# Three new homes for the moving operands of a float32r kernel: 96, 48 and 64 bytes behind a multiple of 128

## The chip, the cores and the metric

The kernel runs on one core of one Trainium2 chip. The metric is the device time of one execution in microseconds, the median of several runs. TensorE's granted clock is read from the profile; its two levels are 1.2 and 2.4 GHz.

## The reference

A stack of four layers over `x` of shape (2, 1024, 256), 2048 tokens of 256 features, with a context of 64 tokens per batch. Each layer is a gated cross attention and a gated feed-forward, both after a layer norm:

```
for layer in 0..3:
    x = x + g_xattn[layer] * cross_attention[layer](layernorm(x), ctx)
    x = x + g_ffn[layer]   * feed_forward[layer](layernorm(x))
```

The feed-forward of layers 0, 2 and 3 is a mixture of 8 experts with 256 -> 1024 -> 256 features (top 1 in layers 0 and 2, top 2 in layer 3), and routes tokens. That of layer 1 runs all 8 experts, each with a gate, an up and a down matrix, over all 2048 tokens. Inputs and outputs are float32.

## The kernel before

All weights of the feed-forwards are split into a high and a low half of type float32r, and so are the tokens and the activations. A float32 product is made of three matmuls in a row: high weights by high tokens, high weights by low tokens, low weights by high tokens. 7200 such matmuls are issued; the weights (128x128) are the stationary operand, and the tokens or activations are the moving operand.

- Layer 1 (`ffn1`): 32 units (8 experts by four quarters of the hidden features), each for two pairs of token blocks, so 64 groups. A group has 14 `product` calls of three matmuls (lines 950 to 952) and four calls of `down` for six matmuls (through the helper `mm`, line 689), 66 matmuls of 512 columns. `product` combines sums of blocks of the tokens with sums of blocks of the weights, seven products in place of eight. The sums of token blocks T2, T3 and T4 stand in `pair_x_rest`; T1 and the plain blocks stand in `xTh` and `xTl` (`x_operand`). `down` reads `h_hi` and `h_lo`.
- Layers 0, 2, 3 (`moe`): 15, 8 and 8 items, each with 8 chunks of the hidden features. A chunk has six matmuls up, which read `xTh`/`xTl`, and six down, which read `h_hi`/`h_lo`, with 256, 384 and 320 columns.

The order on TensorE within a group is written out by hand in `group`: products, `down`, products, `down`, products. PE waits there on semaphores of VectorE (`p_lo`, `p_sum`, `p_y`), ScalarE (`p_act`, `p_copy`) and GpSimd (`p_wup`, `p_wdown`). ScalarE writes `h_hi` (L1491) and VectorE writes `h_lo` (L1939 in layer 1, L2162 in the expert layers). VectorE adds L1926, L1935 (gate and up) and L1948 (the output sum).

All tiles are allocated in one order in each partition of the on-chip memory, each at the next multiple of 32 bytes. Their byte addresses modulo 128, here called homes, follow from that order: `wsplit` (the split weights) starts at 97312, home 32; `moving_home`, a tile of 32 bytes that nothing reads or writes, starts at 172800 (home 0) and pushes `xTh` to 172832; `xTl` follows at 189216, `h_act` at 205600, `h_hi` at 211744, `h_lo` at 219936, all home 32. `pair_x_rest` lies in `wsplit` behind the four blocks of weights, home 32 as well. `xT` stands at home 0 and `sc` at home 0.

Of the kernel before, what the change touches and what calls it, by code (L numbers as in the profile page):

```python
# [11 lines left out]
F32R = mybir.dt.float32r  # L12
# [5 lines left out]
P = 128  # L18
# [7 lines left out]
GT = GROUP * P  # L26
# [15 lines left out]
FH = 4  # L42
QUARTER = F // 4
UNITS = 4 * E
PAIRED = 2 * GT
# [7 lines left out]
UP_COLS, W_COLS = 7 * 2 * P, 7 * 2 * P + 2 * D  # L53
# [17 lines left out]
def build(nc, a, out, subs):  # L71
    with ExitStack() as ctx:
        def sb(name, shape, dt=F32, stack=ctx):
            return stack.enter_context(nc.sbuf_tensor(name, shape, dt))
# [28 lines left out]
        wsplit = sb("wsplit", [P, 16 * PIECE], F32R)  # L103
# [88 lines left out]
            q_inv = asb("q_inv", [P, 2, KD, GT])  # L192
            q_o = asb("q_o", [P, KD, GT])

        sb("moving_home", [P, 8])
        xTh = sb("xTh", [P, KD, T], F32R)
        xTl = sb("xTl", [P, KD, T], F32R)
        h_act = sb("h_act", [P, 2, GT])
        logit_rows = sb("logit_rows", [P, NG, P])
        h_hi = sb("h_hi", [P, FH, GT], F32R)  # L200
        h_lo = sb("h_lo", [P, FH, GT], F32R)

        pair_w = wsplit[:, 0:4 * W_COLS].rearrange("p (s h w) -> p s h w", s=2, h=2)
        pair_up = [[pair_w[:, z, h, 0:UP_COLS].rearrange("p (o m w) -> p o m w", o=7, m=2) for h in range(2)] for z in range(2)]
        pair_down = [[pair_w[:, z, h, UP_COLS:W_COLS].rearrange("p (i d) -> p i d", i=2) for h in range(2)] for z in range(2)]
        pair_x_rest = wsplit[:, 4 * W_COLS:4 * W_COLS + 6 * PAIRED].rearrange("p (h o t) -> p h o t", h=2, o=3)
        lnx_flat = lnx[:, :, :].rearrange("p t d -> p (t d)")
        kept23 = lnx_flat[:, 0:PAIRED].rearrange("p (m t) -> p m t", m=2)
        x_sums = lnx_flat[:, PAIRED:3 * PAIRED].rearrange("p (o t) -> p o t", o=4)
# [2116 lines left out]
```

## Time and profile before

| | |
|---|---|
| median of 3 runs | 1953.7 us (1948.84 to 1954.12) |
| the profiled execution | 1959.86 us |
| its span, first to last instruction | 1958.1 us |
| mean granted TensorE clock | 0.972 |
| TensorE busy | 1828.0 us |
| VectorE, ScalarE, GpSimd busy | 1401.2, 1093.2, 731.4 us |

The span is what the profile's times are counted in. Busy time is the union of an engine's instructions; a matmul's duration reaches from its start to its modelled end and is longer than the distance to the next matmul's start, since they are pipelined. The distance between starts is what a stream of matmuls costs.

### The profile page before, as it was taken

The numbers are of one execution on the slowest core, as the hardware profiler recorded it, in microseconds if no ns is written. First come the engines' busy times: TensorE is split into PE (matmuls) and PEld (weight loads), VectorE is DVE, ScalarE is ACT, GpSimd is POOL, SyncE is SP. The second block draws the span as 40 slices with busy tenths as digits, with TensorE's granted clock in tenths as the row PEclk, the third lists the DMA queues.
The fourth block names the chain that finished last, engine by engine and source line by source line (L and its number), as shares of the span: only waits on it lengthen the run. The fifth ranks groups of instructions, "written<-read, shape, count | busy, mean of one in ns | idle before, by whom it ended". The sixth has DMA issues, their size and how long they took to land.

```text
span 1958.1 us, 34855 instructions
## 1 busy us (share of the span) xinstructions
PE 1828.0 (93%) x11498; PEld 1557.5 (80%) x11498; DVE 1401.2 (72%) x2375; ACT 1093.2 (56%) x2003; POOL 731.4 (37%) x754
## 2 busy tenths in 40 slices
PE   7889997999999999999999999999998997897993
PEld 4579996777888888888888888888767996786993
DVE  4767776778777777777777777777865665766664
ACT  4647774685555555555555555555434773573771
POOL 6024432465354354353443543543002232342231
PEclk8999998999999999999999999999989998899997
DMA  4246663000110000000000100040105442004544
GB/s 127 70 136 193 192 182 98 2 15 19 33 32 16 32 32 17 32 17 32 32 16 32 32 16 32 32 145 27 46 7 168 148 134 87 25 2 130 169 137 143
DMA packets 113578, 138.95 MB, mean 71 GB/s; under 512 B 15332, under 2 KB 101606, under 8 KB 113504
## 3 DMA queue, kind: packets, MB, share of 16 engines
q1 hardware_dynamic: 105952, 121.70, 20.2%
q0 software_dynamic: 7552, 16.24, 2.8%
q8 instruction: 49, 0.80, 0.2%
q14 instruction: 25, 0.20, 0.0%
HBM read 117.22 MB, written 24.90 MB: 73 GB/s over the span
## 4 chain that ended last, share of the span: by engine, by line
PE 82%; DVE 9%; ACT 3%; issue 3%; DMA 2%; SPq 0%; ACTq 0%; POOL 0%; DVEq 0%; another core or an unknown queue 0%; POOLq 0%
PE ps L689 45%; PE ps L950 10%; PE ps L952 10%; PE ps L951 10%; PE ps L696 2%; PE ps L883 1%; PE ps L1150 1%; DVE xs L1800 1%; DVE bn L1720 1%; ACT ps L1596 1%; DVE lnx L1703 1%; PE ps L1109 1%; ACT wsplit L1557 1%; DVE xT L2116 0%; DMA xT<-x_tok,x_idx 0%
## 5 line engine op out<-in xcount | busy, mean ns | idle before, releaser
L689 PE MATMUL ps<-h_hi,wsplit 128*128 128x512 f32 (+3 forms) x2016 | 582.7, 347 | 1.8 <-DVE xT L1948 1.3
L689 PEld LDWEIGHTS ps<-h_hi,wsplit 128*128 128x128 f32 x2016 | 367.5, 189 | 42.5 <-DVE xT L1948 1.7
L689 PE MATMUL ps<-h_lo,wsplit 128*128 128x512 f32 (+3 forms) x1008 | 349.3, 347 | 0.0
L575 POOL TENSOR_TENSOR wsplit<-wraw,zero 128x256 fp32r<-128x256 f32 (+2 forms) x160 | 151.4, 963 | 474.5 <-PE ps L952 394.5
L1478 ACT ACTIVATE lnx<-ps 128x512 f32<-128x512 f32 x384 | 229.3, 598 | 98.8 <-PE ps L952 59.7
L689 PE MATMUL ps<-xTh,wsplit 128*128 128x256 f32 (+2 forms) x992 | 256.0, 312 | 14.8 <-DVE h_lo L2162 12.0
L1487 ACT ACTIVATE h_act<-h_act 128x512 f32<-128x512 f32 x192 | 121.0, 630 | 209.5 <-DVE h_act L1926 209.3
L2162 DVE TENSOR_TENSOR h_lo<-ps,h_hi 128x256 fp32r<-128x256 f32 (+2 forms) x248 | 117.5, 474 | 157.3 <-ACT h_hi L1600 148.4
L1948 DVE TENSOR_TENSOR xT<-xT,ps 128x1024 f32<-128x1024 f32 x124 | 151.4, 1221 | 106.2 <-PE ps L689 106.2
L1491 ACT ACTIVATE h_hi<-ps 128x512 fp32r<-128x512 f32 x256 | 152.6, 596 | 131.1 <-PE ps L689 128.5
L1935 DVE TENSOR_TENSOR ps<-h_act,ps 128x512 f32<-128x512 f32 x256 | 177.5, 694 | 40.2 <-PE ps L952 26.1
L689 PEld LDWEIGHTS ps<-h_lo,wsplit 128*128 128x128 f32 x1008 | 190.1, 189 | 19.9
L636 POOL DMA_INDIRECT y_tok<-xT,y_idx x78 | 89.0, 1141 | 304.0 <-DVE xT L2177 289.7
L950 PE MATMUL ps<-xTh,wsplit 128*128 128x512 f32 x512 | 199.7, 390 | 0.7 <-DVE xTl L1918 0.4
L952 PE MATMUL ps<-xTh,wsplit 128*128 128x512 f32 x512 | 199.2, 389 | 0.0
L951 PE MATMUL ps<-xTl,wsplit 128*128 128x512 f32 x512 | 199.2, 389 | 0.0
L689 PEld LDWEIGHTS ps<-xTh,wsplit 128*128 128x128 f32 x992 | 175.1, 189 | 23.4 <-DVE h_lo L2162 19.4
L1596 ACT ACTIVATE ps<-ps,b1c 128x256 f32<-128x256 f32 (+2 forms) x248 | 120.7, 487 | 105.1 <-PE ps L689 96.6
L1939 DVE TENSOR_TENSOR h_lo<-ps,h_hi 128x512 fp32r<-128x512 f32 x256 | 174.3, 681 | 0.0
L1926 DVE TENSOR_TENSOR h_act<-ps,lnx 128x512 f32<-128x512 f32 x192 | 132.2, 689 | 56.0 <-PE ps L952 48.5
L629 POOL DMA_INDIRECT xT<-x_tok,x_idx x78 | 90.4, 1159 | 200.5 <-DVE x_idx L2121 171.8
L950 PE MATMUL ps<-wsplit 128*128 128x512 f32 x384 | 149.8, 390 | 3.0 <-DVE ps L1926 1.5
(289 smaller groups left out, 3577.6 us busy)
## 6 DMA issues: line engine op xcount, KB each, us to landing
wraw<-in_L_w SPq DMA_DIRECT2D x124, 512.0 KB, 3.7
wraw<-in_L_ffn_Wg SPq DMA_DIRECT2D x32, 256.0 KB, 2.7
wraw<-in_L_ffn_Wu SPq DMA_DIRECT2D x32, 256.0 KB, 3.2
wraw<-in_L_ffn_Wd SPq DMA_DIRECT2D x32, 256.0 KB, 3.6
x_tok<-lnx SPq DMA_DIRECT2D x12, 512.0 KB, 3.8
lnx<-y_tok SPq DMA_DIRECT2D x12, 512.0 KB, 6.2
y_tok<-lnx SPq DMA_DIRECT2D x3, 2048.0 KB, 13.8
wat<-in_attn SPq DMA_DIRECT2D x16, 256.0 KB, 4.8
```

Of the source, the lines that this page charges most:

```text
L575: return pool.tensor_tensor(out_, in_, zero[:, :].to_broadcast(shape), ALU.add)
L689: return pe.matmul(out_, lhsT, rhs, start=start, stop=stop)
L950: pe.matmul(o, w_hi, x_hi, start=fresh, stop=False, skip_group_check=True)
L951: pe.matmul(o, w_hi, x_lo, start=False, stop=False, skip_group_check=True)
L952: pe.matmul(o, w_lo, x_hi, start=False, stop=True, skip_group_check=True).then_inc(p_early if m == 0 and i in (2, 5) else p_up, 1)
L1478: act.activation(dst, ps[:, 3 * m + (1 if i == 2 else 2), :], ACT.Copy).then_inc(p_copy, 1)
L1491: act.activation(h_hi[:, SLOT[c], :], ps[:, H_BANK[c], :], ACT.Copy).then_inc(p_hi, 1)
L1596: act.activation(ps[:, f % 2, 0:cap], ps[:, f % 2, 0:cap], func, bias=b1c[:, layer, bass.ds(ex * FC + f, 1)]).then_inc(m_act, 1)
L1926: dve.tensor_tensor(dst, ps[:, 3 * m, :], kept, ALU.add).then_inc(p_sum, 1)
L1935: dve.tensor_tensor(bank, h_act[:, c in ("12", "21"), :], bank, ALU.mult).then_inc(p_h, 1)
L1939: dve.tensor_tensor(h_lo[:, SLOT[c], :], ps[:, H_BANK[c], :], h_hi[:, SLOT[c], :].bitcast(F32), ALU.subtract).then_inc(p_lo, 1)
L1948: dve.tensor_tensor(xT[:, :, blk], xT[:, :, blk], ps[:, 6:8, :], ALU.add).then_inc(p_y, 1)
```

## The change

A larger tile ahead of `xTh` moves it to 172896, home 96, and with it `xTl`, `h_act` and `logit_rows`. A tile of 32 bytes ahead of the activations brings them to a multiple of 128; `h_hi` and `h_lo` are then allocated 128 bytes larger than their data, and the data starts 48 bytes in. `pair_x_rest` starts 32 bytes later in `wsplit`, home 64. The weights stay at home 32. No instruction, semaphore or transfer differs.

```
-        sb("moving_home", [P, 8])
+        sb("x_home", [P, 24])
         xTh = sb("xTh", [P, KD, T], F32R)
         xTl = sb("xTl", [P, KD, T], F32R)
         h_act = sb("h_act", [P, 2, GT])
         logit_rows = sb("logit_rows", [P, NG, P])
-        h_hi = sb("h_hi", [P, FH, GT], F32R)
-        h_lo = sb("h_lo", [P, FH, GT], F32R)
+        sb("h_home", [P, 8])
+        h_hi, h_lo = (sb(n, [P, 32 + FH * GT], F32R)[:, 12:12 + FH * GT].rearrange("p (f t) -> p f t", f=FH) for n in ("h_hi", "h_lo"))
...
-        pair_x_rest = wsplit[:, 4 * W_COLS:4 * W_COLS + 6 * PAIRED].rearrange("p (h o t) -> p h o t", h=2, o=3)
+        pair_x_rest = wsplit[:, 4 * W_COLS + 8:4 * W_COLS + 8 + 6 * PAIRED].rearrange("p (h o t) -> p h o t", h=2, o=3)
```

## Rows read from the trace of the kernel before

**Rows 1.** The page's header: busy us of each engine.

```profile
span 1958.1 us, 34855 instructions
PE 1828.0 (93%) x11498; PEld 1557.5 (80%) x11498; DVE 1401.2 (72%) x2375; ACT 1093.2 (56%) x2003; POOL 731.4 (37%) x754
```

**Rows 2.** The page: the chain that ended last, by engine and line.

```profile
PE 82%; DVE 9%; ACT 3%; issue 3%; DMA 2%; SPq 0%; ACTq 0%; POOL 0%; DVEq 0%; another core or an unknown queue 0%; POOLq 0%
PE ps L689 45%; PE ps L950 10%; PE ps L952 10%; PE ps L951 10%; PE ps L696 2%; PE ps L883 1%; PE ps L1150 1%; DVE xs L1800 1%; DVE bn L1720 1%; ACT ps L1596 1%; DVE lnx L1703 1%; PE ps L1109 1%; ACT wsplit L1557 1%; DVE xT L2116 0%; DMA xT<-x_tok,x_idx 0%
```

**Rows 3.** Busy time by stretch; the long one is layer 1's feed-forward.

```profile
core 0: us, PE busy (x) PEld busy (x) DVE busy (x) ACT busy (x) POOL busy (x), PEclk, DMA share, GB/s
472.00:1401.70 929.70, 929.70 (x4103) 769.85 (x4102) 713.63 (x995) 497.74 (x870) 396.71 (x417) 1.00 0.10 32
```

**Rows 4.** The chain in order of time (start us, us, what), layer 3; TensorE's timeline, layer 2.

```profile
1820.15 7.04 PE ps L689 x48
...
1520.04 0.33 PE L689 MATMUL ps<-h_lo,wsplit 128*128 128x384 f32 x1
...
1521.25 0.33 PE L689 MATMUL ps<-xTh,wsplit 128*128 128x384 f32 x1
```

**Rows 5.** TensorE's timeline, layer 0: start us, us, operation; 12 matmuls before the last.

```profile
156.13 0.28 PE L689 MATMUL ps<-xTl,wsplit 128*128 128x256 f32 x1
...
157.20 0.28 PE L689 MATMUL ps<-h_lo,wsplit 128*128 128x256 f32 x1
157.32 0.28 PE L689 MATMUL ps<-h_hi,wsplit 128*128 128x256 f32 x1
157.44 0.28 PE L689 MATMUL ps<-xTh,wsplit 128*128 128x256 f32 x1
157.56 0.28 PE L689 MATMUL ps<-xTl,wsplit 128*128 128x256 f32 x1
```

**Rows 6.** TensorE's timeline, attention of layer 0 (plain float32).

```profile
59.67 3.60 PE L689 MATMUL ps<-q_pos,kv 128*128 128x512 f32 x8
63.10 1.04 PE L696 MATMUL ps<-ident 128*128 128x256 bf16 x8
```

**Rows 7.** TensorE's timeline, layer 2 after a break; 5 matmuls before the last.

```profile
1527.45 0.33 PE L689 MATMUL ps<-xTl,wsplit 128*128 128x384 f32 x1
...
1528.34 0.33 PE L689 MATMUL ps<-h_hi,wsplit 128*128 128x384 f32 x1
```

**Rows 8.** TensorE's timeline, layer 1 after a break; each pair 6 matmuls apart.

```profile
470.61 0.39 PE L689 MATMUL ps<-h_lo,wsplit 128*128 128x512 f32 x1
...
472.00 0.39 PE L689 MATMUL ps<-h_lo,wsplit 128*128 128x512 f32 x1
...
1406.26 0.40 PE L689 MATMUL ps<-h_lo,wsplit 128*128 128x512 f32 x1
...
1407.64 0.39 PE L689 MATMUL ps<-h_lo,wsplit 128*128 128x512 f32 x1
```

**Rows 9.** Groups of the stretch 472.0 to 1401.7, by line (busy us, mean ns).

```profile
L689 PE MATMUL ps<-h_hi,wsplit 128*128 128x512 f32 x996 | 326.9, 389 | 0.0
L689 PE MATMUL ps<-h_lo,wsplit 128*128 128x512 f32 x498 | 193.7, 389 | 0.0
L950 PE MATMUL ps<-xTh,wsplit 128*128 128x512 f32 x496 | 192.9, 389 | 0.0
...
L950 PE MATMUL ps<-wsplit 128*128 128x512 f32 x374 | 145.5, 389 | 0.0
```

**Rows 10.** Groups of VectorE and ScalarE, whole span.

```profile
L2162 DVE TENSOR_TENSOR h_lo<-ps,h_hi 128x256 fp32r<-128x256 f32 (+2 forms) x248 | 117.5, 474 | 157.3 <-ACT h_hi L1600 148.4
...
L1491 ACT ACTIVATE h_hi<-ps 128x512 fp32r<-128x512 f32 x256 | 152.6, 596 | 131.1 <-PE ps L689 128.5
...
L1939 DVE TENSOR_TENSOR h_lo<-ps,h_hi 128x512 fp32r<-128x512 f32 x256 | 174.3, 681 | 0.0
...
L2181 DVE TENSOR_TENSOR wsplit<-wraw,wsplit 128x1024 fp32r<-128x1024 f32 x112 | 136.2, 1216 | 0.0
...
L1844 DVE TENSOR_TENSOR sc<-ps,bmask 128x1024 f32<-128x1024 f32 x32 | 39.2, 1224 | 39.0 <-PE ps L689 38.9
```

**Rows 11.** Who waited for whom, in total, times, longest us.

```profile
PE ps L689 <- DVE h_lo L2162: 12.0, 20, 2.2
```

## The prediction

> **What bounds the kernel now.** I read the page's header first. TensorE is busy for 1828.0 us of a span of 1958.1 us, VectorE for 1401.2 us [rows 1]. The chain that ended last says the same: 82% of it is TensorE, and nearly all of that is three groups, the helper line L689 (45%) and the three lines of `product`, L950, L951 and L952 (30% together) [rows 2]. So the question is what one matmul costs, and how many there are.
>
> The table of stretches comes next. In the feed-forward of layer 1, from 472.0 to 1401.7 us, TensorE is busy for 929.70 us of 929.70 us, with 4103 matmuls recorded, at the full granted clock (1.00, the 2.4 GHz level) [rows 3]. One matmul of 512 columns therefore takes 929.70/4103 = 226.6 ns from start to start. 512 columns at 2.4 GHz are 213.3 ns, so there are 13.3 ns on top, the time of 32 columns. The other widths show the same surcharge. In layer 3 (320 columns) the chain has 48 matmuls in 7.04 us, 146.7 ns each, which is 133.3 + 13.3; in layer 2 (384 columns) seven steps take 1521.25 - 1520.04 = 1.21 us, 172.9 ns each, which is 160.0 + 12.9; in layer 0 (256 columns) three steps take 157.56 - 157.20 = 0.36 us, 120 ns each, which is 106.7 + 13.3 [rows 4, 5]. The code issues 4224, 768, 768 and 1440 such matmuls, 7200 in all, about 957 + 133 + 113 + 173 = 1376 us.
>
 There the operands stand at other homes and are taken at half the rate. Between 2.1 and 13.3 ns lie 11.2 ns per matmul.
>
> The surcharge is not rigid either. After a break in the stream it wanders for some matmuls and then comes back to 32 columns. In layer 0, the nine steps from 156.13 to 157.20 us take 1.07 us, 118.9 ns each, shorter than the 120 ns that follow [rows 5]. In layer 2, five steps from 1527.45 to 1528.34 us take 178.0 ns each, longer than 172.9 [rows 7]. At 512 columns, six steps from 470.61 to 472.00 us take 231.7 ns each, and six from 1406.26 to 1407.64 us take 230.0 ns, both longer than 226.6 [rows 8]. So the surcharge depends on how the stream stands in time to something else, and settles where it repeats.
>
> **The change part by part.** All it does is move tiles. By the code, the weights `wsplit` and all moving operands of these 7200 matmuls start 32 bytes behind a multiple of 128 in each partition before; every slice used is a whole number of 128 bytes further on. After it the weights stay at 32, `xTh` and `xTl` go to 96, `pair_x_rest` to 64, `h_hi` and `h_lo` to 48. No instruction, wait or transfer is added, removed or moved: 0 us for instructions, 0 us for queues. `h_act` and `logit_rows` shift with the x halves, to 96.
>
> *TensorE, x halves.* They shift by 64 bytes, 16 columns, half of the 32 that the surcharge measures. No row shows a single precision matmul of this rate at another home, so the price per step is bounded: below by the 2.1 ns of [rows 6], above by the 231.7 ns of [rows 8]. I take 0 within a run of one home.
>
> *TensorE, activations and sums.* They shift by 16 and 32 bytes, and what is new is that neighbouring matmuls have different homes. A group of `ffn1` has 66 matmuls and, going through `group`, 10 changes of home; the experts of layers 0, 2 and 3 change after every six. I take 0 here too: the nearest rows, those of the long stretch by tile, show 389 ns of duration for a matmul (start to end, longer than the step) whether it reads `h_hi`, `h_lo`, `xTh` or the sums in `wsplit`, which lie tens of kilobytes apart [rows 9].
>
> The Trainium skill (SBUF — State Buffer, "Who interferes with whom") gives TensorE two independent read ports, one for the moving operand and one for the weights, and says that it waits for no other engine; by that rule homes would be worth nothing and the sum stays at 0. It also calls 16 bytes the unit of a line, and 96, 64 and 48 are all multiples of it. The Trainium skill (TensorE: Matmul & The Clock Gate, "Wait — 56ns, not 53.3ns?") has a matmul step at its columns over 2.4 GHz plus about 2.5 ns; our plain float32 row agrees with 2.1 ns, the 7200 matmuls here do not, with 13.3 ns.
>
> *VectorE and ScalarE.* They write and read the moved tiles: L1939 at 681 ns and L1491 at 596 ns for 128x512 [rows 10]. On VectorE, 1024 columns take 1216 ns with operands at home 32 (L2181) and 1224 ns at home 0 (L1844) [rows 10], so I take 0. Neither row has a tile at 48. If it cost something, VectorE has 929.70 - 713.63 = 216 us of idle time in the long stretch [rows 3], and the operations cannot reach TensorE there; in the expert layers TensorE waits for L2162 for 12.0 us in all [rows 11], and a tenth more on L2162's 117.5 us [rows 10] would add at most 12 us. At the bottom it is 0, as I know no reason for a gain.
>
> Sum: 0 + 0 + 0 = 0. The profiled execution took 1959.86 us (span 1958.1 and 1.8 around it), 6.2 us above the median of 1953.7; the forecast is made on the median: **1953 us**.
>
> **Rivals.**
> *The homes unlock the stream and it gets faster.* The surcharge is 32 columns at four widths that are all multiples of 64, which is what a stream shows that has to start at a certain point of a repeating pattern, with every start the same address apart. If the weights' reads and the moving reads are what meet, 16, 32 or 64 bytes between them can remove part of the meeting. For it: 118.9 ns in [rows 5] and the 2.1 ns of [rows 6] show that 13.3 is not a floor. Against it: the gain in [rows 5] is small and the other wandering stretches are longer. Price: down to 16 columns saves 6.7 ns, 7200 x 6.7 = 48 us, 1906 us; half way, 3.3 ns, 24 us, **1930 us**. It needs VectorE and ScalarE to keep up, which have slack.
>
> *The homes unlock the stream and it gets slower.* Each change of home disturbs the rhythm as a break does now, and no run is long enough to settle (six or seven steps in [rows 7, 8]; the runs in `ffn1` are 3 to 12 matmuls, those of the experts 6). Then every matmul costs what the wandering stretches cost: 4224 x (230.0 to 231.7 - 226.6) = 14 to 22 us, layer 2 768 x (178.0 - 172.9) = 4 us, layer 0 1440 x (118.9 - 120.0) = -2 us, layer 3 nothing: 16 to 24 us, **1974 us**. It decides once more than about 1.4 ns are added per 512-column step (5.9 us over 4224). For it: [rows 8] twice. Against it: no row ties the wandering to an address.
>
> *The addresses have no effect.* This is the forecast itself; the surcharge would then belong to this type of matmul.
>
> **How the numbers follow.** A measurement of this kernel can tell about 0.3%, 5.9 us, from no change. Chances: no effect, or effects that cancel within that, 0.38; faster 0.35, around 1930 us; slower 0.27, around 1974 us. The two signs are near each other because the rows show a surcharge that can move, and not where to. The likeliest case has a range of its own of 1948 to 1959. The range of 1916 to 1979 leaves out the full 48 us of gain, a little under 0.1, and a loss beyond the priced wandering, about 0.1.
>
> **What would show it.** In the long stretch of layer 1 I expect 226.6 ns per matmul, still no idle time. If homes matter, that quotient moves, and if the changes of home are the cause, single steps at a change from x to h or to the sums differ from those within a run of six. The expert layers should then move per step like layer 1, each by its count: 48 matmuls in 7.04 us in layer 3 is the number to compare. VectorE's 681 ns and ScalarE's 596 ns should stay; if they grow, the tile at 48 is the cause. The prediction is wrong if the surcharge of 32 columns turns out to be made of one shared home.

## The result and the profile after

The changed kernel takes 1963.13 us (1961.96 to 1963.38) against 1953.7 us, a ratio of 1.0058 with an interval of 1.0039 to 1.0077. It is slower: the medians are 9.4 us apart, the ratio makes 11 us of it. The forecast was no change; the case priced as "slower" is the one that came. The time lies inside the stated range.

The page's header and chain of the changed kernel, to be read against [rows 1, 2]:

```profile
span 1961.6 us, 34855 instructions
PE 1835.3 (94%) x11498; PEld 1551.6 (79%) x11498; DVE 1401.6 (71%) x2375; ACT 1094.7 (56%) x2003; POOL 729.9 (37%) x754
...
PE 79%; DVE 10%; ACT 5%; issue 3%; DMA 2%; ACTq 0%; DVEq 0%; POOL 0%; SPq 0%; POOLq 0%
```

The instruction counts are equal. VectorE and ScalarE have the busy time they had, and TensorE is busy for 7.3 us more. The two operations that write the tiles at home 48 did not change either (596 and 681 ns in [rows 10]):

```profile
L1491 ACT ACTIVATE h_hi<-ps 128x512 fp32r<-128x512 f32 x256 | 152.6, 596 | 136.6 <-PE ps L689 131.6
...
L1939 DVE TENSOR_TENSOR h_lo<-ps,h_hi 128x512 fp32r<-128x512 f32 x256 | 174.7, 683 | 0.0
```

The measure for all that follows is one stretch inside layer 1's feed-forward, 500 to 1400 us, which holds nothing but float32r matmuls of 512 columns (two kernels further down are an exception, and it is said there). 900 us divided by the number of matmuls in it is the step. The count takes in one or two matmuls that cross the ends of the stretch, so the quotient is 0.1 to 0.2 ns too small. Busy time by stretch, first the kernel before:

```profile
core 0: us, PE busy (x), PEclk, DMA share, GB/s
500.00:1400.00 900.00, 900.00 (x3973) 1.00 0.10 32
```

and the changed kernel:

```profile
500.00:1400.00 900.00, 900.00 (x3910) 1.00 0.10 32
```

Before, 900/3973 = 226.5 ns; after, 900/3910 = 230.2 ns. TensorE is never idle in either and the granted clock is full (1.00). By the starts of all matmuls in the trace, to the nanosecond, it is 226.7 and 230.3 ns: in columns at 2.4 GHz the surcharge went from 32.0 to 40.7. Over 4224 matmuls that is 4224 x 3.7 = 15 us, and layer 1's feed-forward takes 988.8 us from its first to its last matmul in place of 973.8. The expert layers went the other way. In layer 3 the chain in order of time has 7.01 us for 48 matmuls (7.04 in [rows 4]):

```profile
1877.98 7.01 PE ps L689 x48
```

TensorE's waits for L2162, in total, times, longest us, fell from 12.0 us [rows 11] to 4.6:

```profile
PE ps L689 <- DVE h_lo L2162: 4.6, 14, 0.7
```

From the same starts, the mean surcharge in layer 0 fell from 30.9 to 25.9 columns, 1440 x 5 x 0.417 ns = 3 us, and in layers 2 and 3 by about one column, 0.7 us. 15.4 - 3.7 = 11.7 us, near the measured loss. Not all of the 3.7 us is shown to arrive. A later run, shift64, in which the weights move along with all the moving operands, has the steps of the kernel before in every layer, and there TensorE waits for the same operation, one line further down, for only 3.3 us:

```profile
PE ps L690 <- DVE h_lo L2163: 3.3, 8, 0.7
```

So the fall from 12.0 to 4.6 us is scatter of the profiled execution of before. Layer 0 takes 193.7 us from first to last matmul in the changed kernel, 194.3 us in shift64 and 199.2 us in before. Against shift64 the expert layers together are 1.2 us shorter and layer 1 is 14.9 us longer, 13.7 us in all, which lies within the interval of the ratio as well (8 to 15 us).

Where in layer 1 the time goes shows in TensorE's timeline of the changed kernel:

```profile
900.16 0.39 PE L689 MATMUL ps<-h_hi,wsplit 128*128 128x512 f32 x1
...
902.90 0.40 PE L950 MATMUL ps<-xTh,wsplit 128*128 128x512 f32 x1
...
903.60 0.39 PE L950 MATMUL ps<-wsplit 128*128 128x512 f32 x1
...
904.99 0.40 PE L689 MATMUL ps<-h_hi,wsplit 128*128 128x512 f32 x1
```

Twelve steps of the activations take 902.90 - 900.16 = 2.74 us, 228.3 ns each. The three of x behind them take 233.3 ns each, the six of the sums 231.7 ns each. No kind of operand is at 226.7 ns, not even at the end of a run of twelve: over all 118 such runs of the activations in the stretch the last three steps have 50, 28 and 34 columns, 37.3 on average. So it is not only the change from one home to another that costs.

### The profile page after: what moved, and what is told of

The parts are those of the page before. It is cut to its first block, busy times and chain, and to the rows that moved or that the text cites. A ratio compares the mean times of both kernels' runs of the same rounds, so it can differ in the third digit from the quotient of the medians.

```text
span 1961.6 us, 34855 instructions
## 1 busy us (share of the span) xinstructions
PE 1835.3 (94%) x11498; PEld 1551.6 (79%) x11498; DVE 1401.6 (71%) x2375; ACT 1094.7 (56%) x2003; POOL 729.9 (37%) x754
## 4 chain that ended last, share of the span: by engine, by line
PE 79%; DVE 10%; ACT 5%; issue 3%; DMA 2%; ACTq 0%; DVEq 0%; POOL 0%; SPq 0%; POOLq 0%
PE ps L689 42%; PE ps L952 10%; PE ps L950 10%; PE ps L951 10%; PE ps L696 2%; PE ps L883 1%; ACT ps L1596 1%; ACT wsplit L1557 1%; DVE xs L1800 1%; DVE bn L1720 1%; DVE wsplit L2181 1%; DVE lnx L1703 1%; PE ps L1150 1%; DVE h_lo L2162 1%; ACT h_hi L1600 1%
## 5 line engine op out<-in xcount | busy, mean ns | idle before, releaser
L2162 DVE TENSOR_TENSOR h_lo<-ps,h_hi 128x256 fp32r<-128x256 f32 (+2 forms) x248 | 117.7, 474 | 150.6 <-ACT h_hi L1600 149.6
```

Source lines behind the costliest of these rows:

```text
L2162: dve.tensor_tensor(h_lo[:, f % 4, 0:cap], ps[:, f % 2, 0:cap], h_hi[:, f % 4, 0:cap].bitcast(F32), ALU.subtract).then_inc(f_lo, 1)
```

## The experiments

Each is the kernel before with the edit shown. Homes are byte addresses of the start within a partition; the weights start at 32 unless it says otherwise.

### One part at a time: x96, h48, s64

```
-        sb("moving_home", [P, 8])
+        sb("x_home", [P, 24])
...
+        sb("h_home", [P, 16])
```

> Only xTh and xTl move, from home 32 to 96. The changed kernel shows longer steps in layer 1, about 230 ns against 226.6 ns. Theory A (changes of home): what costs is a neighbour at another home; 8 of the 10 changes of a group stay (x against sums and x against activations), so most of the added 15 us in layer 1 stays, and steps inside a long run of one home go back to 226.6 ns. Theory B (distance from the weights): what costs is how far a moving operand's home lies from the weights' home 32. Then only the x steps are longer, 24 of 66 in a group, about 229 to 231 ns each, the others stay at 226.6 ns, and layer 1 gets longer by 1536 x 3.5 ns = 5 us. Theory C (no effect of x): a shift of 64 bytes is neutral, 226.6 ns everywhere, and the loss came from the other two.

1966.84 us, ratio 1.0086 (1.0056 to 1.0117).

```profile
500.00:1400.00 900.00, 900.00 (x3890) 1.00 0.10 32
```

231.4 ns per step, longer than in the whole change. The run does not decide what it was made for: the filling of 64 bytes ahead of `h_hi` brings it from 211744 to 211872. That is home 32 again modulo 128, but 128 bytes further on, and this turned out to matter (below).

```
-        h_hi = sb("h_hi", [P, FH, GT], F32R)
-        h_lo = sb("h_lo", [P, FH, GT], F32R)
+        sb("h_home", [P, 24])
+        h_hi, h_lo = (sb(n, [P, 32 + FH * GT], F32R)[:, 12:12 + FH * GT] ... for n in ("h_hi", "h_lo"))
```

> Only h_hi and h_lo move, from home 32 to 48. Theory A: 4 changes of home in a group of layer 1 in place of 10, so some 40% of the 15 us, 6 us, and the end of each run of 12 is back at 226.6 ns. Theory B: the h steps alone are longer, 24 of 66, by about 2.5 ns, 1536 x 2.5 = 4 us in layer 1; the x and sum steps stay at 226.6 ns. In layer 0 the gain of the changed kernel (about 2 ns a step) should show for the h steps at least.

1962.54 us, ratio 1.0069 (1.0048 to 1.009).

```profile
500.00:1400.00 900.00, 900.00 (x3931) 1.00 0.10 32
```

229.0 ns per step, 10 us more in layer 1, where theory A gave 6 and theory B 4. Counted modulo 256, `h_hi` stands at 176 and `h_lo` at 48, as in the change. By the starts, the last steps of every run of twelve activations are again 50, 28 and 34 columns, nine and more steps behind the change of home, which theory A alone does not give. The runs of twelve x matmuls have 32.0 columns throughout, but shorter runs of x and sums, which did not move, have up to 54: theory B alone does not give that.

```
-        pair_x_rest = wsplit[:, 4 * W_COLS:4 * W_COLS + 6 * PAIRED]...
+        pair_x_rest = wsplit[:, 4 * W_COLS + 8:4 * W_COLS + 8 + 6 * PAIRED]...
```

> Only the summed blocks move, from home 32 to 64; layers 0, 2 and 3 do not read them. Theory A: 8 changes of home in a group, most of the 15 us. Theory B: the steps of the sums alone are longer, 18 of 66, by about 4.7 ns, 1152 x 4.7 = 5.4 us in layer 1. Both: layers 0, 2 and 3 as before, 120.0, 172.9 and 146.7 ns.

1963.95 us, ratio 1.0074 (1.0046 to 1.0102).

```profile
500.00:1400.00 900.00, 900.00 (x3913) 1.00 0.10 32
```

230.0 ns per step, 14.7 us over 4224. This is the one clean single move of the three, and its timeline shows both mechanisms at once:

```profile
896.17 0.40 PE L950 MATMUL ps<-wsplit 128*128 128x512 f32 x1
...
896.87 0.39 PE L950 MATMUL ps<-xTh,wsplit 128*128 128x512 f32 x1
...
898.03 0.39 PE L952 MATMUL ps<-xTh,wsplit 128*128 128x512 f32 x1
...
899.61 0.40 PE L950 MATMUL ps<-wsplit 128*128 128x512 f32 x1
```

Three steps of the moved sums take 0.70 us, 233.3 ns each. The five steps of x behind them, at home 32 where they always were, take 1.16 us, 232.0 ns each, and the next seven 1.58 us, 225.7 ns each, the 226.7 ns of before within the rounding of the two times: the stream has settled. Over all groups it is the same: in runs of twelve the first five steps have 34 to 54 columns on average, the other seven 32.0. From the starts of all matmuls, 891 steps within runs of the sums carry 16.2 columns above those of before, 6.0 us; the steps that end at x or the activations, which did not move, carry 8.1 us together. 2.2 us of that are steps straight from a matmul with sums to one of them, and can be put down to either. A group has several runs shorter than the five or so steps it takes to settle.

### One home for all: all96, all0, all64

```
-        sb("moving_home", [P, 8])
+        sb("x_home", [P, 24])
...
+        pair_x_rest = wsplit[:, 4 * W_COLS + 16:4 * W_COLS + 16 + 6 * PAIRED]...
```

> All moving operands of the 7200 matmuls at one home again, 96, weights at 32. Theory A: no change of home is left, so every step is as before, 226.6 ns in layer 1, and the time is 1953 us. Theory B: the distance from the weights is 64 bytes for all of them, so every step is longer, about 229 ns in layer 1, 4224 x 2.4 = 10 us more there.

1958.06 us (1955.32 to 1974.12), ratio 1.0044 (1.0031 to 1.0057).

```profile
500.00:1400.00 900.00, 900.00 (x3859) 1.00 0.10 32
```

No change of home is left, and the profiled execution has 233.2 ns per step, 48 columns. Theory A is out as the whole cause. But that execution took 1974.12 us, and the ten others 1955.32 to 1961.41. It was profiled once more:

> The same kernel as all96, profiled again. Its profiled execution took 1974 us at 48 columns per step, but the ten timed ones 1955 to 1961 us. If the stream can settle in more than one pattern, this execution may show the other: the three steps 45, 30, 38 columns (mean 37.7), 229.0 ns, and 4224 x 4.3 ns = 18 us less in layer 1, about 1956 to 1960 us. If every execution is at 48 columns, the two times do not fit together.

1954.71 us, one execution.

```profile
500.00:1400.00 900.00, 900.00 (x3934) 1.00 0.10 32
```

The same program, 228.8 ns per step. From the starts, the first execution steps by 48 columns, the second by 44, 30 and 38 in turn, mean 37.3. The stream can settle in two patterns, 4.4 ns apart, 19 us over the layer, which is the difference of the two executions. The ten others have the time of the second.

```
-        sb("moving_home", [P, 8])
...
+        pair_x_rest = wsplit[:, 4 * W_COLS + 24:4 * W_COLS + 24 + 6 * PAIRED]...
```

> All moving operands at home 0, weights at 32 (distance 96, or -32). If the surcharge grows with distance from 0 (B1), layer 1's steps are longer than 226.6 ns, like the 229 to 233 ns at home 96. If the distance works in both directions and 0 is the worst but for 64, they are shorter.

1976.53 us, ratio 1.0138 (1.012 to 1.0155).

```profile
500.00:1400.00 900.00, 900.00 (x3859) 1.00 0.10 32
```

For all64 the tile ahead of `xTh` has 64 bytes and `pair_x_rest` moves by 8 elements.

> All moving operands at home 64, weights at 32 (distance 32). The sums at home 64 had steps of about 230 ns when they stood alone there. B1 and B2 both expect longer steps than 226.6 ns in layer 1; with one home for all, a single repeated pattern without wandering at each change of operand. Layer 0 tells whether its gain at home 96 is there at 64 too.

1973.44 us, ratio 1.0125 (1.0108 to 1.0143).

```profile
500.00:1400.00 900.00, 900.00 (x3858) 1.00 0.10 32
```

Both have 233.2 to 233.3 ns, 48 columns on average, with unequal steps in both. all64 is a single home for all, and does not bring 226.7 ns back. all0 is one only modulo 128: the sums start at 128 modulo 256 and the x halves and activations at 0, which the next experiments show to be two different places.

### Against the weights or by itself: shift64

```
+        sb("w_home", [P, 16])
         wsplit = sb("wsplit", [P, 16 * PIECE], F32R)
```

> A pad of 64 bytes ahead of the weights moves weights and moving operands together, all to home 96 (everything allocated behind it moves by 64 bytes too). Theory B1 (distance between the moving operand and the weights): the distance is 0 again, so the steps are those of before, 226.6 ns in layer 1, 120.0 ns in layer 0, and the time is that of before within 0.3%. Theory B2 (the moving operand's own home): home 96 costs what it cost with the weights at 32, steps of 229 to 233 ns in layer 1 and about 117.5 ns in layer 0.

1951.8 us, ratio 1.0008 (0.9997 to 1.002).

```profile
500.00:1400.00 900.00, 899.44 (x3972) 1.00 0.10 32
```

All at 96, the weights too, and the step is 899.44/3972 = 226.4 ns. This stretch ends in a short break with six transposes, which the count includes; by the starts the float32r matmuls are 226.7 ns apart, 32.0 columns as before. Home 96 costs nothing where the weights stand there as well, and with the weights at 32 it cost 228.8 or 233.2 ns (all96). What counts is the distance between the moving operand and the weights (B1), not the place (B2).

### Expert layers apart from layer 1: split_e96

```
+        x_raw = [sb(n, [P, 32 + KD * T], F32R) for n in ("x_raw_hi", "x_raw_lo")]
+        xTh, xTl = (v[:, 0:KD * T]... for v in x_raw)
+        eTh, eTl = (v[:, 16:16 + KD * T]... for v in x_raw)
```

and the same for `h_hi` and `h_lo`; the expert layers use the second views.

> Layer 1 reads and writes its tiles at home 32 as before, the expert layers 0, 2 and 3 use the same memory 64 bytes further on, at home 96, weights at 32. With all of them at 96 the expert layers were shorter from first to last matmul, 199.2 to 193.5 us, 146.2 to 143.9 us and 125.6 to 123.6 us, and layer 1 was longer. If the home counts by width as read there, this keeps the gain of 10 us and has 226.6 ns in layer 1: about 1940 us, a ratio of 0.995. If the gain of the expert layers came from the neighbourhood of layer 1's home, or is scatter between executions, no change.

1956.8 us, ratio 1.0036 (1.0024 to 1.0049).

```profile
500.00:1400.00 900.00, 900.00 (x3944) 1.00 0.10 32
```

Not the gain of 10 us but a loss. The surprise is layer 1: all its operands stand at home 32, and the step is 228.2 ns. The 128 bytes of padding in each tile had moved `xTl` and `h_lo` to 160 modulo 256, while `h_hi` and `xTh` stayed at 32. The expert layers had their low halves at 224 and their high halves at 96 for the same reason, so they were not the test that was meant either.

### 128 or 256: h160, hlo160, all160, split256

```
+        sb("h_home", [P, 32])
         h_hi = sb("h_hi", [P, FH, GT], F32R)
```

> A pad of 128 bytes ahead of h_hi moves h_hi and h_lo by 128 bytes: home 32 as before when one counts modulo 128, but 160 modulo 256; everything else as before. In the run with split views, layer 1 had all homes at 32 modulo 128 and still left the 226.6 ns; its low halves stood at 160 modulo 256. Theory P128 (addresses count modulo 128): 226.6 ns at every step in layer 1, the time of before. Theory P256 (they count modulo 256): the h steps are longer, mean surcharge 36 to 48 columns in place of 32, 2 to 7 ns, for 1536 of the steps, 3 to 10 us.

1960.76 us, ratio 1.0044 (1.0027 to 1.006).

```profile
500.00:1400.00 900.00, 900.00 (x3927) 1.00 0.10 32
```

For hlo160 the same tile stands between `h_hi` and `h_lo`.

> Only h_lo moves by 128 bytes, to 160 modulo 256, h_hi stays at 32. P128: as before. P256: the step behind or at a matmul with h_lo changes, in a repeated pattern of three (as 52, 28, 33 columns in the run with split views, mean 37.7 against 32), 1536 x 2.4 = 3.6 us in layer 1.

1955.68 us, ratio 1.0024 (1.0009 to 1.0038).

```profile
500.00:1400.00 900.00, 900.00 (x3959) 1.00 0.10 32
```

For all160 the tile ahead of `xTh` has 160 bytes and `pair_x_rest` moves by 32 elements.

> All moving operands 128 bytes further on, 160 modulo 256, with the weights at 32. P128: as before, 226.6 ns in layer 1. P256: a distance of 128 from the weights, with one pattern for all; if the surcharge grew with the distance it is longer than at 96 (37 to 48 columns), about 48 columns, 233 ns, 1965 to 1978 us.

1977.06 us, ratio 1.0116 (1.0093 to 1.0138).

```profile
500.00:1400.00 900.00, 900.00 (x3875) 1.00 0.10 32
```

229.2, 227.3 and 232.3 ns: three kernels whose homes modulo 128 are those of before, and none has its step. P128 is out. By the starts, hlo160 has 32.0 columns at every step of x and sums, and 32, 50 and 30 in turn in the activations, the only ones with a moved half. The fourth execution of all160 took 1969.02 us against 1976.93 to 1977.8, and was not profiled.

```
-        x_raw = [sb(n, [P, 32 + KD * T], F32R) for n in ("x_raw_hi", "x_raw_lo")]
+        x_raw = [sb(n, [P, 64 + KD * T], F32R) for n in ("x_raw_hi", "x_raw_lo")]
```

> The split views again, now with tiles padded by 256 bytes, so that layer 1 has all its operands at 32 modulo 256 and the expert layers theirs at 96 modulo 256. P256: layer 1 is back at 226.6 ns per step, which the run with 128 bytes of padding had lost (231.0 by its 36 columns... 228.3 ns), and the expert layers keep a mean surcharge of 25 columns in layer 0 in place of 31: 1440 x 2.5 ns = 3.6 us at best, so 1947 to 1951 us against 1950. P128: layer 1 as in the first split run, 36 columns.

1948.92 us (1945.49 to 1953.46), ratio 0.9983 (0.9972 to 0.9995).

```profile
500.00:1400.00 900.00, 898.97 (x3973) 1.00 0.10 32
```

With 256 bytes of padding layer 1 is back at 898.97/3973 = 226.3 ns, with the views in place (this stretch reaches over a break at the end of layer 1 with sixteen transposes, which the count includes; ahead of it the step is 226.7 ns by the starts, 32.0 columns). So it was the 128 bytes. The kernel is 0.17% faster than before, the only one here below it, and beats the changed kernel by 0.75%. Layer 0 has a surcharge of 23.9 columns in place of 30.9, 1440 x 7 x 0.417 = 4.2 us at most. 3.3 us arrive in the time of the whole kernel, but from first to last matmul layer 0 is only 1.0 us shorter than in shift64 (193.3 and 194.3 us), so where the rest comes from is not shown.

### The parts without the 128 bytes: x96c, h48c, after_c

In x96c `xTh` and `xTl` stand at 96, and the filling ahead of `h_hi` has 192 bytes, so that the activations are at 32 modulo 256.

> x halves at 96, activations and sums at 32, all counted modulo 256. In the first x96 run the filling ahead of h_hi brought the activations to 160 modulo 256, and their steps were 44 columns long in place of 32; this run takes that out. If only addresses and the settling after a change count: the h steps settle towards 32 within a run of 12 (mean 35 to 38), the x steps stay at about 38 to 41, and layer 1 is 8 to 12 us longer in place of 19.6.

1964.16 us, ratio 1.0072 (1.0055 to 1.0088).

```profile
500.00:1400.00 900.00, 900.00 (x3908) 1.00 0.10 32
```

230.3 ns, 1.1 ns less than x96, 16 us in layer 1 where 8 to 12 were expected. From the starts, h steps within a run have 38.5 columns (44.3 in x96), x steps 43.3.

```
+        h_hi, h_lo = (sb(n, [P, 64 + FH * GT], F32R)[:, 4:4 + FH * GT] ... for n in ("h_hi", "h_lo"))
```

> Only the activations move, both halves at 48 modulo 256. In the change as made, the padding of 128 bytes put h_hi at 176 and h_lo at 48. If the distance of the one half counts, the steps of h differ from those of the first h48 run (40 columns, in threes of 50, 28, 35). 16 bytes from the weights: either near 32 columns, if a small distance is harmless, or 38 to 48.

1962.9 us, ratio 1.0063 (1.0046 to 1.008).

```profile
500.00:1400.00 900.00, 900.00 (x3927) 1.00 0.10 32
```

229.2 ns: 16 bytes from the weights for both halves cost as much as the 144 and 16 of h48. A small distance is not harmless. after_c joins both with the sums at 64:

> The change as it was meant, modulo 256: x at 96, sums at 64, both activation halves at 48. If the 128 bytes between h_hi and h_lo are a part of the loss, layer 1 is nearer to before than the 988.8 us of the changed kernel (973.8 before), by up to the 7 us that the h steps cost there; if the loss is the distances of x and sums and the settling, it is 985 to 990 us again.

1965.32 us, ratio 1.0076 (1.0059 to 1.0093).

```profile
500.00:1400.00 900.00, 900.00 (x3896) 1.00 0.10 32
```

231.0 ns against 230.2 of the changed kernel. The accidental 128 bytes between the halves of the activations did not make the change worse; without them it is as slow or a little slower. The parts do not add up: x 16 us, the activations 11, the sums 15, all three 19 in this form, since every one of them already makes most of the stream wander.

## Why the prediction was wrong

**The bound and the count.** Right. TensorE's step carried the effect, the instructions are equal, and in the long stretch the step moved with no idle time.

**"TensorE, x halves ... I take 0 within a run of one home."** This step failed. A shift of 64 bytes against the weights makes the surcharge 37 or 48 columns in place of 32 at 512 columns (all96, two executions), with no change of home in the stream. Half of 128 is no neutral shift there; of the shifts tried at 512 columns only the joint one of all operands was.

**"TensorE, activations and sums ... the nearest rows show 389 ns whatever is read."** This step failed as a reading. [Rows 9] compares tiles tens of kilobytes apart, but `wsplit` and all of them start at 32 modulo 256. They could not show what another distance costs, since they all have the same. The row that did bear on it was [rows 8], where the step is 230.0 to 231.7 ns with every home as it was.

**The rule on ports.** The Trainium skill (SBUF — State Buffer, "Who interferes with whom") has two independent read ports for TensorE. The runs do not bear out that homes are then worth nothing: with the weights and the moving operands both shifted by 64 bytes (shift64) the step is 226.7 ns, with the moving operands alone shifted by the same 64 bytes (all96) it is 228.8 or 233.2 ns. Which part of the memory or the engine ties the two reads together is not shown here; only their addresses and the step are.

**VectorE and ScalarE.** Right at 0: 683 and 596 ns.

**The rival that came.** "Slower" was priced with 14 to 22 us in layer 1; it measured 15. Its mechanism, a change of home disturbs the rhythm like a break, is shown in s64 by steps of operands that had not moved, 232.0 ns and then 225.7 ns. It is only half of the story: in s64 6 to 8 of 14 us, and the rest is the distance itself, which the rival did not have. That its price for layer 1 came out is therefore partly luck. It also said that no run is long enough to settle; the runs of twelve are, in s64 after five steps and in x96c after seven. Its total of 1974 us was too high because the layer of 256 columns gained up to 3 us in place of 2, layer 2 lost nothing in place of 4 us, and layer 1 stood at the lower end.

**The rival of gain.** Its mechanism, fewer meetings with the weights' reads, exists at 256 columns (25.9 columns of surcharge after, 23.9 in split256). At 512 columns none of the placements tried, fourteen with the change itself, had a mean below 32.

**What would show it.** The quotient of layer 1 moved, as the text asked for. That the expert layers would then move per step like layer 1 did not hold: they went the other way. And the 32 columns are made of one shared home in a sense that the text did not have: at 512 columns sharing it with the weights gives the smallest surcharge found, not the largest.

**The sum against one execution.** The profiled execution of before was 6.2 us above the median, and layer 0 was a part of that: 199.2 us from first to last matmul there, 194.3 us in shift64 with the same surcharge of 30.9 columns, and 193.3 to 194.3 us in all the other profiled kernels. The 10 us of gain expected from split_e96 came from that comparison, and were mostly scatter.

Not settled: why the surcharge is 32 columns at distance 0, why the same distance acts differently at each width, and what decides between the two patterns of all96.

## What to carry to other kernels

When float32r matmuls of 512 columns follow each other without a gap, keep moving operands and weights at the same address modulo 256 bytes, and pad tiles by multiples of 256. For other widths measure anew: at 256 columns here a distance of 64 bytes was better. Measure the step in a stretch without idle time, matmuls per microsecond, since it resolves about 0.05% where a run's time scatters by 0.3%. Take more than one profile of a program before trusting its pattern: all96 had two. Tiles that share a property cannot show that the property does not matter: before taking 0 from equal rows, look up whether they differ in what is changed.

## What the runs showed of the hardware

- A float32r matmul of 512 columns started 226.7 ns after the one before it where the distance to the weights was 0 modulo 256 (before, shift64, split256), and 233.3, 228.8 or 233.2, and 232.3 ns at uniform distances of 32, 64 and 128 (all64, all96, all160). all0, with 224 for x and activations and 96 for the sums, had 233.2 ns. The Trainium skill (TensorE: Matmul & The Clock Gate, "Wait — 56ns, not 53.3ns?") has the columns over the clock plus about 2.5 ns; that holds in this case for plain float32 ([rows 6]: 2.1 ns, and 2.5 ns by the starts to the nanosecond), not for float32r.
- At 256 columns the order is another: a mean of 30.9 columns of surcharge in layer 0 at distance 0, 24.5 to 24.9 at 64. At 320 and 384 columns a uniform distance of 64 changed nothing: behind the first dozen steps of each unbroken run there are 32.0 columns in all96 as in shift64. At 128 (all160) it was 32.0 at 320 columns and 38.1 at 384.
- After a matmul at another distance or after a break the stream took some steps to come back to 32 columns where the operands stood at distance 0: five in s64, seven in x96c, at 512 columns.
- One program can settle in two patterns for a millisecond: 233.2 and 228.8 ns per step in two executions of all96, 19 us apart.
